# Order of gathers, products, tower steps and loads in an interaction network on one core

## What is computed

```python
x0 = e                                     # (1024, 32, 16)
xk = x0
outs = []
for W in (W0, W1, W2):                     # (32, hk_prev, 64)
    xk = relu(einsum('bmd,bhd,mhk->bkd', x0, xk, W))
    outs.append(sum(xk, axis=2))
h = concatenate([concatenate(outs, 1), dense_ctx], 1)      # 192 + 16
h = maximum(h @ W_top1 + b_top1, 0)        # 208 -> 512
h = maximum(h @ W_top2 + b_top2, 0)        # 512 -> 256
y = h @ W_top3                             # 256 -> 1
```

## Time and profile before

| | us |
|---|---|
| median of 3 runs | 698.55 (698.49 to 698.56) |
| the profiled execution | 699.1 |
| its span in the profile | 697.3 |
| busy: TensorE, VectorE | 581.6, 569.7 |
| busy: GpSimd, ScalarE | 453.7, 231.7 |
| moved by DMA | 151.95 MB, 218 GB/s over the span |

### The profile page before, as it was taken

One profiled execution on the slowest core, in us unless ns is written; L12 is line 12 of the kernel. 1 busy time (PEld: TensorE's weight loads), 2 busy tenths in 40 slices (PEclk: granted clock), 3 DMA queues, 4 the chain that ended last, 5 costly groups with the idle time before them and its releaser, 6 DMA issues.

```text
span 697.3 us, 7219 instructions
## 1 busy us (share of the span) xinstructions
PE 581.6 (83%) x2752; PEld 199.7 (29%) x2752; DVE 569.7 (82%) x295; ACT 231.7 (33%) x425; POOL 453.7 (65%) x348
## 2 busy tenths in 40 slices
PE   0040788999899989999899979998999989999978
PEld 0010222223332323323332324232332333233424
DVE  0020899998899998898889898898889889999963
ACT  0100361433325162615224242616243331616031
POOL 6776016188966978487948888487948896636120
PEclk9995799999999999999999999999999999999989
DMA  5498639059591949368672949195855949193000
GB/s 152 153 392 313 259 136 351 1 174 363 174 360 36 379 151 378 127 213 324 249 285 90 398 129 394 63 329 206 310 224 158 377 148 386 24 384 124 1 0 0
DMA packets 54244, 151.95 MB, mean 218 GB/s; under 512 B 9697, under 2 KB 18913, under 8 KB 54210
## 3 DMA queue, kind: packets, MB, share of 16 engines
q1 hardware_dynamic: 46018, 149.39, 57.1%
q0 software_dynamic: 8192, 2.11, 2.4%
HBM read 147.26 MB, written 4.20 MB: 217 GB/s over the span
## 4 chain that ended last, share of the span: by engine, by line
POOL 43%; issue 29%; PE 17%; DVE 3%; ACT 3%; POOLq 2%; SPq 1%; DMA 1%; DVEq 0%
POOL emb L281 25%; POOL zg L293 18%; PE acc L474 15%; DVE zd L360 3%; POOLq L292 2%; ACT xk_sb L389 1%; ACT xk_ps L389 1%; DMA z2d_y<-dense_t_in 1%; PE mlp L515 1%; ACT relu_ab L396 0%; PE mlp L506 0%; PE mlp L507 0%; PE acc L482 0%; DVE zpart L340 0%; PE mlp L562 0%
## 5 line engine op out<-in xcount | busy, mean ns | idle before, releaser
L360 DVE TENSOR_TENSOR zd<-rolled,xk_ps 128x2048 f32<-128x2048 f32 x244 | 543.9, 2282 | 112.5 <-issue 41.8
L474 PE MATMUL acc<-zd,w_sb 128*64 128x512 f32 x1696 | 401.0, 605 | 60.1 <-issue 33.5
L293 POOL TENSOR_TENSOR zg<-rolled,xk_sb 128x1024 f32<-128x1024 f32 x88 | 208.9, 2379 | 152.9 <-ACT xk_sb L389 151.8
L281 POOL DMA_INDIRECT emb<-tables_in,index x256 | 244.5, 955 | 69.2 <-issue 64.6
L474 PEld LDWEIGHTS acc<-zd,w_sb 128*64 128x64 f32 x1696 | 116.3, 138 | 317.7 <-issue 218.9
L389 ACT ACTIVATE xk_ps<-acc 64x512 f32<-64x512 f32 x128 | 73.0, 570 | 104.9 <-issue 52.9
L474 PE MATMUL acc<-zg,w_sb 128*64 128x512 f32 x352 | 91.4, 597 | 14.9 <-POOL zg L293 14.4
L474 PE MATMUL acc<-zd,w 128*64 128x512 f32 x256 | 63.0, 612 | 37.4 <-issue 36.7
L389 ACT ACTIVATE xk_sb<-acc 64x512 f32<-64x512 f32 x128 | 75.7, 591 | 3.1
L396 ACT ACTIVATE relu_ab<-acc 128x512 f32<-128x512 f32 x48 | 28.7, 597 | 122.7 <-issue 72.1
L474 PEld LDWEIGHTS acc<-zg,w_sb 128*64 128x64 f32 x352 | 23.8, 136 | 70.7 <-POOL zg L293 35.6
(11 more groups left out here) (46 smaller groups left out, 69.9 us busy)
## 6 DMA issues: line engine op xcount, KB each, us to landing
rolled<-x_scratch SPq DMA_DIRECT2D x256, 512.0 KB
base<-x_scratch SPq DMA_DIRECT2D x16, 512.0 KB
emb<-tables_in,index POOLq DMA_INDIRECT x256
x_scratch<-emb SPq DMA_DIRECT2D x32, 128.0 KB
w_sb<-w_in SPq DMA_DIRECT2D x2, 512.0 KB
wt<-wtop_in SPq DMA_DIRECT2D x1, 512.0 KB
wt1a<-wtop_in SPq DMA_DIRECT2D x1, 256.0 KB
w<-w0a_in SPq DMA_DIRECT2D x1, 160.0 KB
```

What stands on the lines that cost most here:

```text
L281: pool.indirect_dma_start(emb[:, i % 2, c * DIM:(c + 1) * DIM], None, tables, bass.IndirectOffsetOnAxis(index[:, g:g + 1].bitcast(U32), 0) ...
L293: nc.gpsimd.tensor_tensor(zg[:, n % ZG_BUFS, :], rolled[:, s, j, :], xk_sb[:, s, :], ALU.mult).then_inc(zg_ready, 1)
L360: nc.vector.tensor_tensor(zd[:, n % ZD_BUFS, 0:w, :], rolled[:, s, j:j + w, :], repeated(xk_ps[:, s, :], w), ALU.mult).then_inc(zd_ready, 1)
L474: end = nc.tensor.matmul(acc[h * MAPS:(h + 1) * MAPS, s, :], weights, z[:, h * HALF:(h + 1) * HALF], start=(i == 0 and c == 0), stop=(i == ...
```

## The change

1. **Gathers.** 32 ahead of everything, not 51. The five ahead of k1 are gone. Behind each product of GpSimd in k1, k2, k4, k5 now stand 2 or 3 gathers, 4 behind the last of k2 and 5 behind the last of k5; the first streams have (0,1) with 2 and 6.
2. **GpSimd's chunks.** k1, k2, k4, k5 had 2, 4, 4, 2 and have 2, 4, 2, 4. In the first streams (0,1), (0,2), (1,1) had 0, 0, 2 and have 2, 2, 4. In all GpSimd makes 94 chunks, not 88, and VectorE 241 products, not 244.
3. **Tower steps.** `zsum` stands behind k2, not inside; `mlp2` in k5 behind its first item, not at two thirds; `mlp3` inside k5 at two thirds, not behind it. ScalarE takes z behind k2's evacuation; y ahead of k5's. `base_to_ps` of a stream now is tied to the phase two ahead, which is the same place as before.
4. **Loads.** Chunk j covers shifts 1 + j + 4g (g = partition modulo 4), not BASES[j] + g, so that two neighbouring chunks are neighbouring rows: a load moves two chunks in runs of 8 KB, eight loads per stream of 1 MB each, with one semaphore per pair. They are issued in the order in which both chunks of a pair come free.

```diff
-BASES = [1, 5, 9, 13, 0, 2, 3, 4, 6, 7, 8, 10, 11, 12, 14, 15]
+FIRST_BASE = 1
+STEP = 4
+LOAD = 2
-POOL_CHUNKS = {(0, 0): 0, (1, 0): 0, (0, 1): 4, (1, 1): 2, (0, 2): 4, (1, 2): 2}
-POOL_CHUNKS_FIRST = {(0, 0): 0, (1, 0): 0, (0, 1): 0, (1, 1): 2, (0, 2): 0, (1, 2): 2}
+POOL_CHUNKS = {(0, 0): 0, (1, 0): 0, (0, 1): 4, (1, 1): 4, (0, 2): 2, (1, 2): 2}
+POOL_CHUNKS_FIRST = {(0, 0): 0, (1, 0): 0, (0, 1): 2, (1, 1): 4, (0, 2): 2, (1, 2): 2}
-GATHERS_FIRST = 51
-GATHERS_BEFORE = 5
-GATHERS_AFTER = {1: [4, 5], 2: [1, 1, 1, 5], 4: [3, 1, 1, 1], 5: [2, 2]}
+GATHERS_FIRST = 32
+GATHERS_AFTER = {(1, 2): [2, 3], (0, 1): [2, 2, 2, 4], (0, 2): [2, 2], (1, 1): [3, 3, 2, 5]}
+GATHERS_AFTER_FIRST = {(1, 2): [2, 3], (0, 1): [2, 6], (0, 2): [2, 2], (1, 1): [3, 3, 2, 5]}
...
+def load_order(users):
+    def freed(j):
+        return max([k for k, (_, _, first, w) in enumerate(users) if first < j + LOAD and j < first + w], default=j)
+    return sorted(range(0, NCH, LOAD), key=freed)
...
-                order = PLAN.merged[phase_of(i - 2, 2) if i > 1 else phase_of(i, 1)]
-                for who, n, first, w in order:
-                    if i > 1:
-                        sp.wait_ge(zd_ready if who == "dve" else zg_ready, n + 1)
-                    for j in range(first, first + w):
-                        sp.dma_start(rolled[:, s, j, :], rows_from(BASES[j], i, 1)).then_inc(rolled_in[s][j], 16)
+                users = PLAN.merged[phase_of(i - 2, 2)] if i > 1 else []
+                for j in load_order(users):
+                    for who, n, first, w in users:
+                        if first < j + LOAD and j < first + w:
+                            sp.wait_ge(zd_ready if who == "dve" else zg_ready, n + 1)
+                    sp.dma_start(rolled[:, s, j:j + LOAD, :], rows_from(FIRST_BASE + j, i, STEP, LOAD)
+                                 ).then_inc(rolled_in[s][j // LOAD], 16)
...
-                if q < len(ORDER) - 1:
-                    if k == 2:
-                        zsum_to_sb(m)
-                    if k == 4:
-                        h1_to_sb(m)
-                    if k == 5:
-                        h2_to_sb(m)
-                evacuate(q)
-                if k == 5:
-                    y_to_sb(m)
-                if layer == 2 and stream + 2 < STREAMS:
-                    base_to_ps(stream + 2)
+                if k == 4:
+                    h1_to_sb(m)
+                if k == 5:
+                    h2_to_sb(m)
+                    y_to_sb(m)
+                evacuate(q)
+                if k == 2:
+                    zsum_to_sb(m)
+                if q + 2 < len(ORDER) and ORDER[q + 2][1] == 0:
+                    base_to_ps(ORDER[q + 2][0])
...
-                phase(q + 2, lambda: zsum(m))
+                phase(q + 2)
+                zsum(m)
                 phase(q + 3)
-                phase(q + 4, lambda: mlp1(m))
-                phase(q + 5, lambda: mlp2(m))
-                mlp3(m)
+                phase(q + 4, late=lambda: mlp1(m))
+                phase(q + 5, early=lambda: mlp2(m), late=lambda: mlp3(m))
```

More of the change, by code:

```diff
@@ L173, in build_cin_tower @@
         base_in = sem("base_in")
-        rolled_in = [[sem(f"rolled_{'ab'[s]}{j}_in") for j in range(NCH)] for s in range(2)]
+        rolled_in = [[sem(f"rolled_{'ab'[s]}{j}_in") for j in range(NCH // LOAD)] for s in range(2)]
         base_ps = sem("base_ps")
@@ L224, in store_scratch, with rows_from @@
                         "f (g c) -> (f g) c", g=GROUPS), emb[:, i % 2, :]).then_inc(scratch_in[i % 2], 16)
-            def rows_from(first, i, step):
+            def rows_from(first, i, step, w):
                 return bass.AP(scratch.tensor, scratch.offset + (i * ROWS + first) * COLS,
-                               [[COLS, FIELDS], [step * COLS, GROUPS], [1, COLS]])
+                               [[COLS, FIELDS], [step * COLS, GROUPS], [1, w * COLS]])
             def load_stream(i):
@@ L306, in _ @@
             gathers(GATHERS_FIRST)
-            for q in range(len(ORDER)):
-                k = (q - HEAD) % 6
-                if q >= HEAD and k == 0:
-                    gathers(GATHERS_BEFORE)
+            for q, (stream, layer) in enumerate(ORDER):
                 if PLAN.pool[q]:
@@ L315, in _ @@
                     product(q, n, j)
-                    if k in GATHERS_AFTER:
-                        gathers(GATHERS_AFTER[k][x])
+                    gathers((GATHERS_AFTER if stream > 1 else GATHERS_AFTER_FIRST)[stream % 2, layer][x])
         @block.vector
@@ L356, in _ @@
                         dve.wait_ge(zd_used, n - ZD_BUFS + 1)
-                    for c in range(j, j + w):
-                        if layer == 0 or (layer == 1 and c >= L0CH):
+                    if layer == 0 or (layer == 1 and j >= L0CH):
+                        for c in range(j // LOAD, (j + w - 1) // LOAD + 1):
                             dve.wait_ge(rolled_in[s][c], 16 * (stream // 2 + 1))
@@ L419, in _ @@
             base_to_ps(0)
-            evacuate(0)
-            base_to_ps(1)
-            for q in range(1, len(ORDER)):
-                stream, layer = ORDER[q]
+            for q in range(len(ORDER)):
                 k = (q - HEAD) % 6 if q >= HEAD else None
@@ L458, in _, with phase @@
         def _(pe):
-            def phase(q, between=None):
+            def phase(q, **between):
                 stream, layer = ORDER[q]
@@ L483, in phase @@
                                              xk_sb[:, s, h * HALF:(h + 1) * HALF], start=False, stop=False)
-                    if between is not None and i == len(merged) * 2 // 3:
-                        between()
+                    if "early" in between and i == 0:
+                        between["early"]()
+                    if "late" in between and i == len(merged) * 2 // 3:
+                        between["late"]()
             def half_sums(m, dst, layer):
@@ L539, in _ @@
                 phase(q + 1)
-                phase(q + 2, lambda: zsum(m))
+                phase(q + 2)
+                zsum(m)
                 phase(q + 3)
-                phase(q + 4, lambda: mlp1(m))
-                phase(q + 5, lambda: mlp2(m))
-                mlp3(m)
-            phase(len(ORDER) - 1, last_sums)
+                phase(q + 4, late=lambda: mlp1(m))
+                phase(q + 5, early=lambda: mlp2(m), late=lambda: mlp3(m))
+            phase(len(ORDER) - 1, late=last_sums)
             m = TILES - 1
@@ L574, in layout @@
     p = np.arange(P)
-    base = np.array(BASES)
-    m = (base[:, None] + p[None, :] % 4 + p[None, :] // 4) % FIELDS
+    base = FIRST_BASE + np.arange(NCH)
+    m = (base[:, None] + STEP * (p[None, :] % 4) + p[None, :] // 4) % FIELDS
     h = np.broadcast_to(p % MAPS, m.shape)
```

4 lines of the change are left out of this document (2 added, 2 removed).

## The result

| | before | after |
|---|---|---|
| median of the runs, us | 698.52 (697.98 to 698.56, 4 runs) | 672.14 (670.5 to 677.65, 4 runs) |
| the profiled execution, its span | 699.1, 697.3 | 672.73, 670.9 |

The ratio is 0.9638, 95% interval 0.9582 to 0.9694: faster, by 26 us, inside the range of 645 to 682 and 15 us above the forecast of 657. The runs of the changed kernel also lie further apart (7 us) than those before (0.6 us).

The account below looks back on a forecast made before the run. Bound by handovers, no single engine (TensorE 83%, VectorE 82% busy). Span 697.3, head -29.7, six periods -12.7, last period +0.9, gives 655.8; the median lies 1.25 above the span, so 657; range 645 to 682, its own 650 to 664.

Parts of the forecast that it names:

- half two: The stretch from k5's end to the next k2's end, forecast at 35.9 us, was 36.6.
- edit 1: At the start, 32 gathers first end ahead of TensorE's phase (0,0), so ScalarE starts at 44.1, not 68.50: 24.4 us.
- rest of the head: Up to (1,1)'s end, forecast 29.7 us earlier in all; beside the stall, TensorE's slow clock costs VectorE 0.8 us.
- edit 2: At the start, GpSimd takes more chunks in (0,1), (0,2), (1,1), sparing VectorE 3 products, 6.6 us.
- half one: The stretch from k2's end to k5's end, forecast at 38.9 us, was 40.3.
- tail: The 31 us behind the last period, forecast to stay.
- Edit 3: In half two, the MLP sums behind k2 lie in TensorE's 1.2 us wait and cost nothing: 35.9 us, was 36.6.
- Edit 4: In half one, GpSimd's chunks go two to k4, four to k5, last layer inside: 38.9 us; h2 ready at 33.8, just when wanted.
- the chain is late by 3 us, 675, or half of it, 666: Rival: in half one the gather, store, base, h2, last layer chain is late, 6 x 3 = 18 us; chance 0.14.
- covered, by 2 us: Stream 2t+1's load: first chunks land at +30, wanted at +32.8, the next at +33, wanted at +35.
- Slower by 8 KB runs: Rival: loads in 8 KB runs go at 15 bytes per ns and engine, 37 us a stream, about 727; chance 0.04.
- The page on queues: At the start, 8 KB runs would hold gathers and stores up, perhaps 2 us on stream 1: 659 instead of 657.

Follow-up runs that it names:

- e2: The changed kernel with 16 gathers in the first run instead of 32, and 24 instead of 8 behind the two products of (0,1); 687.85 us.
- e3: The kernel before, its 51 gathers first kept, with loads from stream 0's fifth chunk on held back until TensorE's count of phase (0,0); 705.73 us.
- e6: The changed kernel with the old split, four GpSimd chunks in k4 and two in k5, the same 17 gathers behind them; 684.69 us.
- e8: e4 with the first run of gathers cut from 32 to 27, the other five of stream 1 behind ScalarE's first copy; 663.96 us.
- e12: The changed kernel with 27 gathers first, seven behind ScalarE's first copy, later gathers in GpSimd's gaps, mlp2 late in k5, mlp3 and y behind it; 654.42 us.
- e9: The changed kernel with four more gathers behind the two products of phase (0,2), 4 and 4 instead of 2 and 2; 668.57 us.
- e4: The changed kernel with ScalarE taking h2 ahead of the base copy at the end of half one, not behind it; 668.77 us.
- e5: The changed kernel with one chunk in each load again, runs of 4 KB instead of 8 KB; 669.37 us.
- e1: The changed kernel with 51 gathers first instead of 32, so fewer behind the products of (0,1), (0,2) and (1,1); 687.05 us.
- e7: The changed kernel with the tower steps put back: sums inside k2, second layer late in k5, third behind k5; 669.16 us.

## Why the prediction was right, step by step

The direction, the cause of the late start and half two came out; the forecast was 15 us low. The measured 672 misses the forecast's own range, 650 to 664. It lies inside the stated one because that was held open up to 682 for rivals, one of which, at 666 to 675, came true in part. By its own terms, against the span of 655.8 that it gave and the 670.9 measured:

| term | predicted | measured | difference |
|---|---|---|---|
| stall at the start (edit 1) | -24.4 | -20.1 | +4.3 |
| rest of the head (clock, edit 2) | -5.3 | -5.2 | +0.1 |
| seven half twos | 251.3 | 253.3 | +2.0 |
| seven half ones | 271.9 | 280.4 | +8.5 |
| tail | 31 | 31.1 | +0.1 |

**Edit 1.** The reading was right: ScalarE waited for an increment of TensorE that the gathers delayed, and e2 and e3 show that they do it alone, where the prediction had still written "a long run of gathers beside a load". The size was wrong in one step: "the run ends at 42.9, ahead of TensorE's end", so no stall. The run ended at 42.7, about as forecast, and TensorE at 42.43, earlier than the 44.0 reckoned with. But e6 shows that even an end at 45.10, some 2.3 us behind the run on GpSimd, is not enough: ScalarE starts at 48.29 there. With 27 gathers the wait is gone (0.03 us in e8, 0.04 in e12), and in e12 the 4.3 us with it: ScalarE starts at 43.91.

**Edit 2.** 6.6 us for three products, less what clock and TensorE's order cost, fits: beside the stall the head lost 0.1 us against the sum. No run takes the products and the clock apart.

**Edit 3.** 35.9 us for half two, 35.78 seen, by the arithmetic of TensorE's items. The first one is 2.5 us longer, for VectorE starts phase (2,0) at 106.21 with 3.89 us of waiting for the load. The prediction had it there at 99: stream 2's sixteenth gather came 4.0 us later than reckoned (92.54, not 88.5), with the stall, and its first chunks took 13.7 us from there, not 10.5.

**Edit 4.** The 38.9 us of half one are the floor: 39.06 with nothing late (e9); where the 0.16 lie is not shown. The step that failed was its slack. The prediction wrote 33.8 against 33.8, "no slack is left", and then took zero wait as the value. A chain of gather, store, base, copy and h2 with no slack can only lose, and it lost 1.0 us in the mean, 2.5 once. Half one's +8.5 us are 1.5 for the floor (7 x 39.06 = 273.4 against 271.9) and 7.0 for the chain, of which e4 took away 5.8 and e9 all. The rival "the chain is late by 3 us, 675, or half of it, 666" described this case better than the forecast did: what happened was a third of it, together with the rest of the stall. The prediction also checked the odd stream's load against VectorE's first two pairs alone ("covered, by 2 us"). GpSimd, which now makes four chunks of k5, wants its first one at +14.5 of half one, and waited 2.65 us for it at 389.44; that is what made the chain late in the worst half.

**Slower by 8 KB runs.** It did not come: 401 and 384 GB/s in loads, against 375 and 377 in the earlier trace rows.

**The page on queues.** The Trainium skill (DMA: Bandwidth & Descriptors, Queues, rings and completion order) says that an engine drains a whole packet of one queue before it turns to another. That 8 KB runs would therefore hold up gathers and stores more than 4 KB runs is the prediction's inference, and the traces don't bear it out in any size that counts here. From the store at the start to base's issue, beside a load, it took 6.7 us in the kernel before and 7.1 in e5 with 4 KB, and 5.0 to 7.3 us with 8 KB (5.0 in the changed kernel, 7.3 in e1, 6.8 in e4, 7.1 in e6, 6.7 in e7, 5.9 in e9). A gather beside the load landed 4.7 to 4.9 us behind its start in the kernel before between 36 and 47 us, and 4.9 to 5.2 in the changed one, 0.3 us more. The 2 us that the prediction would have added are not there.

## What to carry to other kernels

A chain that is computed to come out at zero slack has to be charged with a part of its possible lateness, or be taken off the path: here the order of two copies on ScalarE, or four gathers one phase earlier, bought what all of part 3 lost. A layer that hangs on a DMA chain should stand behind the phase, not inside it. When work is spread over gaps, look at every product behind it: the same four gathers cost 6 us in (0,2) and nothing in places where GpSimd was waiting anyway.
